# Projecting raw rows with centred weights, and applying 1/std afterwards, in a fused layer-norm, attention and expert kernel

## Chip, cores and metric

One core of a Trainium2 chip. The metric is the device time of one execution in microseconds (us). TensorE (PE) multiplies matrices and turns tiles, VectorE (DVE), ScalarE (ACT) and GpSimd (POOL) work on elements, SyncE (SP) issues most transfers.

## What is computed

The input is 8 sequences of 512 rows of 128. Each row is normalised; attention with 16 heads of 8 (causal, with a mask that depends on distance and head) and a mixture of 8 experts of which each row uses 2 are added to the row. Cut to what matters:

```python
def _layernorm(x, axis=-1, eps=1e-05):
    m = jnp.mean(x, axis=axis, keepdims=True)
    v = jnp.var(x, axis=axis, keepdims=True)
    return (x - m) / jnp.sqrt(v + eps)
...
qkv = x @ w_attn
...
logw = -jnp.log1p(decay[:, None, None] * log1p_dist)
attn_mask = causal[None, :, :] + logw
scores = jnp.einsum('bhqd,bhkd->bhqk', q, k) * (1.0 / jnp.sqrt(jnp.float32(D)))
att = jax.nn.softmax(scores + attn_mask[None], axis=-1)
...
logits = jnp.einsum('btd,ed->bte', x, Wr)
topk_vals, topk_idx = jax.lax.top_k(probs, TOPK)
h = jax.nn.silu(jnp.einsum('btd,efd->btef', x, W1))
...
xn = _layernorm(x, axis=-1)
x = x + attn(xn, ...) + ffn(xn, W1, W2, Wr)
```

## The kernel before

The rows lie in 32 tiles of 128, four to a batch. The attention works through 32 groups (8 batches of 4 groups of 4 heads) in a software pipeline of slots: `slot_steps(n)` lists the steps of slot n in one order, and each engine runs those that it has a function for, in that order. `PROLOGUE` is the list ahead of slot 0; `EARLY` and `EARLY_1` weave its remainder into slots 0 and 1, behind the score products of the group. Nothing else orders the engines but semaphores.

Steps by their two letters, with the lines that do them:

- BN, RS: mean and variance of tiles (VectorE, L942 and after), then 1/std as a power on GpSimd (L727), in three parts: batch 0, batches 1 to 3, batches 4 to 7.
- NX, NP: normalised rows `xn_all`, by VectorE for batches 0 and 4 to 7 (L959), by GpSimd for 1 to 3 (L734). The expert part sends these rows too.
- XB, VL: four normalised tiles of a batch are turned (L1210), copied by ScalarE (L815), and projected to values and expert logits (L1223), which ScalarE and VectorE copy (L820, L981). VS and XS store values and turned rows to DRAM; LC copies the logits (L741).
- KA, QA: keys and queries of a whole batch (L1250), split into three bf16 parts by ScalarE and VectorE (KR, KL, KM and the same with Q), written to DRAM (KW, QW) and loaded group by group (KD, QD), all of that on SP's queue.
- LN, CZ: the mask of a head, a logarithm on ScalarE (L809), and its causal edge for four heads on GpSimd (L748). The scores of group g wait for CZ g in the first four groups.
- P1: the score products of a group in ten units (L1266); VectorE takes the mask off and finds the row maximum (L1121); GpSimd subtracts for six units (L765) and ScalarE for the other four (SA, L846).
- TE: in slot n PE turns the ten units of group n - 1 (L1291) and ScalarE takes the exponentials (L884). `psT` has two buffers, so a turn waits for the exponential two before it. PV (L1309) multiplies with the values in slot n + 2 of group n, V brings the next batch's values (L870), OT, YT and PJ finish a batch.
- R1 to R17: choice of experts on VectorE in slots 2 to 12; SC sends rows to their expert's place on GpSimd (L776), the first choice in slots 8 to 18, the second in 20 to 30, three tiles a slot. MI, MU, MD run the 71 expert tiles behind the last slot.

## Time and profile before

| | |
|---|---|
| median of three runs | 531.16 us (529.22 to 532.96) |
| the profiled execution | 531.62 us, span 529.8 us, mean granted clock 0.974 |
| busy, share of the span | PE 91%, VectorE 68%, POOL 64%, ACT 63% |
| chain that ended last | PE 72%, VectorE 18%, POOL 3%, DMA 2%, ACT 2% |

Span is the stretch from the first to the last instruction on the profile; the 1.8 us beside it are the run's own. A group of instructions is given by source line, engine, operation, tile written and read, shape and count, with busy time and mean duration; a timeline row is start, duration, engine, line, operation and count, and in brackets the idle time before it with what released it. PEclk is the granted TensorE clock as a share of full speed.

### The profile page before, as it was taken

Reading aid. Unit: us, or ns where it says so; the run is one execution under the profiler, and the core shown is the slowest. Engines: PE = TensorE matmul, PEld = TensorE weight load, DVE = VectorE, ACT = ScalarE, POOL = GpSimd, SP = SyncE. Lnnn points to the kernel's source line nnn. Section 1 sums busy time; section 2 is a strip of 40 time slices with the busy share of each in tenths; the row PEclk is TensorE's granted clock in tenths of the full one; section 3 lists DMA queues with packets and bytes.
Section 4 is the critical chain, followed back from the end, with each engine's and each line's share of the span. In section 5 each row is a group of like instructions: output and inputs, shape, how many; then the busy total and the mean of one; then the engine's idle time right before and its main releaser. Section 6 shows DMA issues by size and latency. Waiting matters only on the chain.

```text
span 529.8 us, 13373 instructions
## 1 busy us (share of the span) xinstructions
PE 482.3 (91%) x4316; PEld 351.6 (66%) x4316; DVE 360.5 (68%) x1406; ACT 335.6 (63%) x600; POOL 338.4 (64%) x566
## 2 busy tenths in 40 slices
PE   7767999989999999999999999999999999999920
PEld 6545566555565665665565565666999999999910
DVE  7595997988988878888878878872433333333326
ACT  3578878878878878878878878776232333333300
POOL 2873555556888878876878888970454555555524
PEclk9988999999999999999999999999999999999975
DMA  6566591570460451450460451355466677666449
GB/s 179 168 232 207 156 219 47 157 214 8 136 185 23 135 173 36 137 164 23 136 181 27 137 165 50 107 171 141 121 201 190 209 215 207 207 183 207 131 166 319
DMA packets 71826, 80.38 MB, mean 152 GB/s; under 512 B 8638, under 2 KB 52672, under 8 KB 71760
## 3 DMA queue, kind: packets, MB, share of 16 engines
q1 hardware_dynamic: 67440, 71.06, 45.8%
q0 software_dynamic: 4320, 8.47, 4.5%
q8 instruction: 38, 0.62, 0.5%
q14 instruction: 28, 0.23, 0.1%
HBM read 48.11 MB, written 31.84 MB: 151 GB/s over the span
## 4 chain that ended last, share of the span: by engine, by line
PE 72%; DVE 18%; POOL 3%; DMA 2%; ACT 2%; issue 2%; SPq 0%; DVEq 0%; ACTq 0%; POOLq 0%
PE psT L1291 22%; PE psO L1309 13%; PE ps L1336 12%; DVE scores L1121 12%; PE psT L1363 12%; PE ps L1266 7%; PE psM L1250 2%; POOL xn_all L734 2%; DVE x_all L535 2%; PE ps L1327 1%; PE psM L1320 1%; DMA probs<-picked_dram 1%; POOL rstd L727 1%; ACT probs L884 1%; DMA decay_in<-decay_raw 1%
## 5 line engine op out<-in xcount | busy, mean ns | idle before, releaser
L1121 DVE CUSTOM_DVE_ANT_0 scores<-ps,wdist 128x256 f32<-128x256 f32 (+3 forms) x512 | 218.6, 486 | 28.1 <-PE ps L1266 25.4
L765 POOL TENSOR_SCALAR scores<-scores,row_max 128x256 f32<-128x256 f32 (+2 forms) x384 | 177.5, 477 | 62.9 <-DVE row_max L1121 61.6
L884 ACT ACTIVATE probs<-psT 128x512 f32<-128x512 f32 x320 | 173.7, 594 | 54.8 <-PE psT L1291 54.4
L1291 PE MATMUL psT<-ident,scores 128*128 128x128 f32 x1280 | 177.2, 281 | 3.4 <-ACT probs L884 2.8
L1291 PEld LDWEIGHTS psT<-ident,scores 128*128 128x128 f32 x1280 | 137.6, 141 | 63.7 <-issue 37.5
L783 POOL DMA_INDIRECT picked_dram<-scores,row_ring x71 | 69.7, 982 | 80.6 <-DVE scores L1173 79.1
L893 ACT ACTIVATE scores<-ps 128x512 f32<-128x512 f32 x71 | 42.4, 597 | 95.1 <-PE ps L1336 95.1
L846 ACT ACTIVATE scores<-scores,row_max 128x512 f32<-128x512 f32 x128 | 84.8, 714 | 0.0
L1309 PE MATMUL psO<-probs,values 128*32 128x512 f32 (+3 forms) x1024 | 82.0, 438 | 0.0
L1336 PE MATMUL ps<-scores,wdist 128*128 128x128 f32 x568 | 75.3, 276 | 0.8 <-DVE scores L1161 0.8
L1363 PE MATMUL psT<-wdist,scores 128*128 x568 | 75.3, 276 | 0.6 <-ACT scores L893 0.6
L776 POOL DMA_INDIRECT rows_dram<-xn_all x64 | 63.3, 989 | 16.2 <-issue 16.2
L1336 PEld LDWEIGHTS ps<-scores,wdist 128*128 128x128 f32 x568 | 69.1, 192 | 1.6 <-DVE scores L1161 1.2
L1363 PEld LDWEIGHTS psT<-wdist,scores 128*128 128x128 f32 x568 | 69.0, 192 | 1.1 <-issue 1.0
L1266 PE MATMUL ps<-k_rows,q_rows 48*128 48x256 bf16 (+3 forms) x512 | 57.8, 302 | 6.2 <-DVE row_max L1121 3.8
L1161 DVE COPY scores<-ps 128x128 f32<-128x128 f32 x71 | 20.6, 291 | 52.0 <-PE ps L1327 52.0
L1173 DVE TENSOR_SCALAR scores<-psT,row_ring 128x128 f32<-128x128 f32 x71 | 24.9, 351 | 43.8 <-PE psT L1363 43.8
L1309 PEld LDWEIGHTS psO<-probs,values 128*32 128x32 f32 x1024 | 25.5, 109 | 37.7 <-issue 28.5
L1121 DVE DVE_READ_ACCUMULATOR2_ANT row_max<- 128x1 f32 x512 | 42.1, 82 | 0.0
L1266 PEld LDWEIGHTS ps<-k_rows,q_rows 48*128 48x128 bf16 x512 | 17.1, 94 | 32.4 <-DVE row_max L1121 16.6
L1327 PE MATMUL ps<-ident,row_ring 128*128 128x128 f32 x71 | 19.2, 273 | 0.1
L535 DVE TENSOR_TENSOR x_all<-x_all,probs 128x512 f32<-128x512 f32 x12 | 11.1, 927 | 8.5 <-DMA probs<-picked_dram 8.1
(140 smaller groups left out, 277.4 us busy)
## 6 DMA issues: line engine op xcount, KB each, us to landing
wdist<-w1t SPq DMA_DIRECT2D x71, 256.0 KB, 3.2
k_rows<-k_dram SPq DMA_DIRECT2D x64, 96.0 KB, 2.8
q_rows<-q_dram SPq DMA_DIRECT2D x64, 96.0 KB, 2.6
row_ring<-rows_dram SPq DMA_DIRECT2D x71, 65.0 KB, 3.0
probs<-picked_dram SPq DMA_DIRECT2D x8, 512.0 KB, 6.8
rows_dram<-row_ring SPq DMA_DIRECT2D x7, 585.0 KB, 5.8
k_dram<-k_parts SPq DMA_DIRECT2D x7, 384.0 KB, 2.3
q_dram<-q_parts SPq DMA_DIRECT2D x7, 384.0 KB, 2.6
```

Source lines behind the costliest of these rows:

```text
L765: last = nc.gpsimd.tensor_scalar(part, part, -1.0, row_max[:, r, tile, quad:quad + 1], ALU.mult, ALU.add)
L776: nc.gpsimd.indirect_dma_start(out=rows_dram, out_offset=bass.IndirectOffsetOnAxis(ap=xn_all[:, t, 0:1].bitcast(U32), axis=0), in_=xn_all[ ...
L783: nc.gpsimd.indirect_dma_start(out=picked_dram, out_offset=bass.IndirectOffsetOnAxis(ap=slot_rows[s % RING][:, 0:1].bitcast(U32), axis=0), ...
L846: nc.scalar.activation(part, part, ACT.Identity, scale=-1.0, bias=row_max[:, r, TILES - 1, quad:quad + 1]).then_inc(less_act, 1)
L884: nc.scalar.activation(probs[:, at.ring(2), w, :], psT[:, w % 2], ACT.Exp, scale=-1.0).then_inc(exp_ready, 1)
L893: nc.scalar.activation(hidden_t[:, s % 2], ps1[:, s % 2], ACT.Silu).then_inc(hidden_ready, 1)
L1121: last = nc.vector.tensor_tensor_reduce(out=scores[:, r, u, col:col + n], in0=bank[:, col:col + n], in1=wdist[:, at.g * QUADS + quad, SEQ ...
L1266: last = mm(ps1[:, 2 * (step % 2) + strip, col:col + n], q_rows[a:a + HEAD_ROWS, at.ring(4), pair, tile * P:n], k_rows[a:a + HEAD_ROWS, at ...
L1291: last = nc.tensor.transpose(psT[:, w % 2, place * P:(place + 1) * P], scores[:, at.ring(2), u, col + key * P:col + (key + 1) * P], ident[:])
L1309: last = mm(psO[quad * QROWS:(quad + 1) * QROWS, tile * P:], values[:, at.parity, tile, first:first + QROWS], probs[:, at.ring(2), unit, a ...
L1336: last = mm(ps1[:, s % 2, f * P:(f + 1) * P], slot_w1[s % RING][:, f * P:(f + 1) * P], slot_xt[:, s % 2], start=True, stop=True)
L1363: last = mm(psT[:, s % 2, 0:C], hidden_t[:, s % 2, f * P:(f + 1) * P], w2[:, bass.ds(start + f * C, C)], start=(f == 0), stop=(f == FT - 1))
```

## The change

The rows of batches 1 to 7 are no longer normalised before they are turned and projected. The weights (now one array with the expert router's) are centred once: PE multiplies them by identity minus 1/128 (WC), which takes the mean off every row that is projected. 1/std comes in as a factor later: turned rows are multiplied by a broadcast row of it on VectorE (XN) before keys and queries; values when ScalarE brings them in (four instructions, one a tile); logits on GpSimd in LC. For that, 1/std is turned on PE (RT), copied, stored to DRAM (RO) and loaded back for all partitions into `yt` (RB). The rows for the experts are normalised on GpSimd in slots 3 to 8, five tiles a slot (NR), and the sends begin in slot 9.

With it: projections get banks of their own (`vl_banks`), six of eight projections stand in the prologue, the second query write moves to GpSimd's queue (QP), GpSimd subtracts all ten units in slots 0 to 2, and logarithms 8 to 15 move behind the third score product of slots 1 and 2. The table of `log_dist` moves to the last part of `probs`, which is why the last exponential of slot 2 waits for all masks. Core of the diff:

```diff
...
-FIRST_SEND_SLOT = 8
...
-EARLY = {0: (("VL", 12), ("LN", 4), ("LN", 5)),
-         1: (("NX", 16), ("VS", 12), ("LC", 4), ("LN", 6), ("LN", 7), ("CZ", 1)),
-         2: (("XB", 16), ("XS", 16), ("NX", 20), ("LC", 8), ("LN", 8), ("LN", 9)),
-         3: (("VL", 16), ("XB", 20), ("XS", 20), ("VS", 16), ("NX", 24), ("LC", 12), ("LN", 10), ("LN", 11), ("CZ", 2)),
-         4: (("VL", 20), ("XB", 24), ("XS", 24), ("VS", 20), ("NX", 28), ("LC", 16), ("LN", 12), ("LN", 13))}
-EARLY_1 = (("VL", 24), ("XB", 28), ("XS", 28), ("VS", 24), ("LC", 20), ("LN", 14), ("LN", 15), ("CZ", 3), ("VL", 28),
-           ("VS", 28), ("LC", 24), ("LC", 28))
+EARLY = {0: {1: (("VL", 24), ("LN", 4), ("LN", 5)),
+             2: (("VL", 28), ("LN", 6), ("LN", 7)) + tuple(("LC", b * GROUPS) for b in range(6)),
+             3: (("RT", 1), ("V0", 0), ("XN", 4), ("LC", 24), ("LC", 28), ("CZ", 1)),
+             4: tuple((kind, b * GROUPS) for kind, b in (("VS", 4), ("VS", 5), ("XS", 3), ("VS", 6), ("VS", 7), ("XS", 4))
+                      ) + (("RO", 1), ("XS", 20), ("XS", 24), ("XS", 28))},
+         1: {2: (("LN", 8), ("LN", 9)), 3: (("LN", 10), ("LN", 11), ("CZ", 2))},
+         2: {2: (("LN", 12), ("LN", 13)), 3: (("LN", 14), ("LN", 15), ("CZ", 3))}}
+FIRST_ROWS_SLOT, ROW_TILES = 3, 5
...
+GROUPS_BY_POOL = 3
...
+def act_units(c):
+
+    return ACT_UNITS if c >= GROUPS_BY_POOL else ()
...
+    per_batch("XT", -4)
+    per_batch("RB", -4)
...
-    step("SA", n, NGROUP, (0, 1))
+    if n >= GROUPS_BY_POOL:
+        step("SA", n, NGROUP, (0, 1))
...
-    per_batch("XT", -4)
     p1(4)
+    per_batch("XN", -4)
     step("TE", n - 1, NGROUP, 8, 10)
-    step("SA", n, NGROUP, (6, 7))
+    if n >= GROUPS_BY_POOL:
+        step("SA", n, NGROUP, (6, 7))
+    first = TILES + ROW_TILES * (n - FIRST_ROWS_SLOT)
+    if TILES <= first < NTILE:
+        steps.append(("NR", 0, first, min(NTILE, first + ROW_TILES)))
...
 PROLOGUE = [
-    ("BN", 0, 0, 0, 4), ("RS", 0, 0), ("NX", 0), ("WU", 18), ("XB", 0), ("KA", 0), ("QA", 0), ("WU", 16),
-    ("BN", 0, 1, 4, 16), ("RS", 0, 1), ("NP", 4), ("NP", 8), ("NP", 12),
-    ("KR", 0), ("QR", 0), ("KM", 0), ("QM", 0), ("LN", 0), ("LN", 1),
-    ("KL", 0), ("QL", 0), ("KW", 0, 0), ("QW", 0, 0), ("KD", 0), ("QD", 0), ("KW", 0, 1), ("QW", 0, 1),
-    ("VL", 0), ("XB", 4), ("LN", 2), ("LN", 3), ("CZ", 0),
-    ("BN", 0, 2, 16, 20), ("BN", 0, 2, 20, 24), ("VL", 4), ("XB", 8), ("XS", 8),
-    ("BN", 0, 2, 24, 28), ("VL", 8), ("XB", 12), ("XS", 12), ("BN", 0, 2, 28, 32), ("RS", 0, 2),
-    ("V0", 0), ("VS", 4), ("VS", 8), ("LC", 0)]
-MISC_KINDS = ("KA", "QA", "VL", "PJ", "CT")
+    ("BN", 0, 0, 0, 4), ("RS", 0, 0), ("WU", 10), ("WC", 0), ("WU", 6), ("NX", 0), ("XB", 0), ("XB", 4), ("KA", 0), ("QA", 0),
+    ("BN", 0, 1, 4, 16), ("RS", 0, 1),
+    ("KR", 0), ("QR", 0), ("KM", 0), ("QM", 0), ("KL", 0), ("QL", 0), ("XB", 8), ("VL", 0),
+    ("KW", 0, 0), ("QW", 0, 0), ("KD", 0), ("QD", 0), ("QP", 0),
+    ("XB", 12), ("VL", 4), ("RT", 0), ("LN", 0), ("LN", 1), ("BN", 0, 2, 16, 20),
+    ("XB", 16), ("VL", 8), ("LN", 2), ("LN", 3), ("CZ", 0), ("BN", 0, 2, 20, 24),
+    ("XB", 20), ("VL", 12), ("BN", 0, 2, 24, 28),
+    ("XB", 24), ("VL", 16), ("BN", 0, 2, 28, 32), ("RS", 0, 2),
+    ("XB", 28), ("VL", 20),
+    ("RO", 0), ("KW", 0, 1), ("RB", 4), ("VS", 4), ("VS", 8), ("XS", 8), ("VS", 12)]
+MISC_KINDS = ("KA", "QA", "PJ", "CT")
...
+        def vl_banks(b):
+
+            if b > 5:
+                return psO, psM
+            return (ps1[:, 0], ps1[:, 1]) if b % 2 == 0 else (psO, ps1[:, 3])
...
-                sp.dma_start(w_qkv[:, 0:3 * C], w_attn).then_inc(w_loaded, 16)
+                sp.dma_start(w_qkv[:], w_attn).then_inc(w_loaded, 16)
...
-                    if n == 0:
-                        sp.dma_start(w_qkv[:, 3 * C:], wrt).then_inc(consts_dma, 16)
...
+                def rstd_store(at):
+                    n = at.c
+                    sp.wait_ge(rstd_copied, n + 1)
+                    sp.dma_start(rstd_dram[n * NTILE // 2:(n + 1) * NTILE // 2], rstd_stage(n)).then_inc(rstd_stored, 16)
+
+                def scales_load(at):
+                    b = at.c // GROUPS
+                    sp.wait_ge(rstd_stored, 16 if b < 4 else 32)
+                    if b == 2:
+                        sp.wait_ge(xt_scaled, 1)
+                    if b >= 3:
+                        sp.wait_ge(misc_full, at.misc_before("PJ", 3 * GROUPS, 1))
+                    sp.dma_start(yt[:], rstd_dram[b * TILES:(b + 1) * TILES].rearrange("(a t) p -> a (t p)", a=1
+                                                                                     ).broadcast_to([P, SEQ])
+                                 ).then_inc(scales_loaded, 16)
...
-                    elif at.g == 0 or at.c == 1:
-                        sp.wait_ge(q_written, at.batches(48, 48))
+                    elif at.c == 1:
+                        sp.wait_ge(q_by_pool, 48)
+                    elif at.g == 0:
+                        sp.wait_ge(q_written, at.batches(48))
...
+                pool.wait_ge(ident_ready, 1)
+                nc.gpsimd.tensor_scalar(centre, ident[:], 1.0, -1.0 / C, ALU.mult, ALU.add).then_inc(centre_ready, 1)
...
-                def normalise_step(at):
...
+                def rows_step(at, first, end):
+
+                    for t in range(first, end):
+                        nc.gpsimd.tensor_scalar(xn_all[:, t, 3:], x_all[:, t, :], mean[:, t:t + 1], rstd[:, t:t + 1],
+                                                ALU.subtract, ALU.mult).then_inc(rows_normal, 1)
...
+                    pool.wait_ge(rstd_ready, 3)
+                    scale = rstd[:, b * TILES:(b + 1) * TILES].rearrange("p (t a) -> p t a", a=1)
+                    nc.gpsimd.tensor_tensor(dst, v_stage(b)[:, :, C:], scale.broadcast_to([P, TILES, EXPERTS]), ALU.mult
+                                            ).then_inc(logits_ready, 1)
...
+                def queries_write(at):
+                    write_queries(nc.gpsimd, pool, at, 1, q_by_pool)
...
+                run_prologue({"RS": rstd_step, "QP": queries_write, "CZ": causal_step})
...
+                        pool.wait_ge(rows_normal, NTILE - TILES)
...
+                def centred_copy(at):
+                    act.wait_ge(centred_full, 1)
+                    nc.scalar.activation(w_qkv[:], ps1[:, 0, 0:3 * C + EXPERTS], ACT.Copy).then_inc(centred_copied, 1)
...
+                    act.wait_ge(rstd_ready, 3)
...
-                    nc.scalar.activation(value_cols[:, at.parity, :, :, 0:HD],
-                                         v_back[:, :, 0:C].rearrange("p t (h d) -> p t h d", d=HD),
-                                         ACT.Copy).then_inc(values_ready, 1)
+                    for t in range(TILES):
+                        tile = at.batches(TILES, t)
+                        last = nc.scalar.activation(value_cols[:, at.parity, t, :, 0:HD],
+                                                    v_back[:, t, 0:C].rearrange("p (h d) -> p h d", d=HD),
+                                                    ACT.Copy, scale=rstd[:, tile:tile + 1])
...
+                        if at.c == 1 and w == UNITS - 1:
+                            act.wait_ge(wdist_ready, HEADS)
...
+                def scaled_weights(at):
+                    dve.wait_ge(centred_copied, 1)
+                    v.tensor_scalar(w_q[:], w_qkv[:, 0:C], SCALE, None, ALU.mult).then_inc(w_q_ready, 1)
...
+                def scale_tokens(at):
+
+                    b = at.c // GROUPS
+                    dve.wait_ge(scales_loaded, 16 * b)
+                    if b == 1:
+                        dve.wait_ge(xt_copied, 2)
+                        dve.wait_ge(vl_full, 2)
+                    else:
+                        dve.wait_ge(xt_loaded, 16 * (b - 1))
+                    v.tensor_tensor(xt[:, at.parity, :], xt[:, at.parity, :], yt[:], ALU.mult).then_inc(xt_scaled, 1)
...
+                    dve.wait_ge(rows_normal, at.batches(TILES))
...
-                    if b in POOL_NORMS:
...
+                    if b == 0:
+                        pe.wait_ge(xn_ready, 1)
...
-                        pe.wait_ge(xn_ready, 1 if b == 0 else b - 2)
+                        pe.wait_ge(x_loaded[b // TILES], 16)
...
-                        last = nc.tensor.transpose(xt_bank(b)[:, t * P:(t + 1) * P], xn_all[:, b * TILES + t, 3:], ident[:])
+                        tile = xn_all[:, t, 3:] if b == 0 else x_all[:, b * TILES + t, :]
+                        last = nc.tensor.transpose(xt_bank(b)[:, t * P:(t + 1) * P], tile, ident[:])
...
+                def centre_weights(at):
+
+                    pe.wait_ge(centre_ready, 1)
+                    pe.wait_ge(w_loaded, 16)
+                    mm(ps1[:, 0, 0:3 * C + EXPERTS], centre, w_qkv[:], start=True, stop=True).then_inc(centred_full, 1)
...
+                def rstd_turn(at):
+
+                    n = at.c
+                    pe.wait_ge(rstd_ready, n + 2)
+                    pe.wait_ge(vo_free, BATCH if n else 2)
+                    nc.tensor.transpose(psO[0:NTILE // 2, SEQ - P:], rstd[:, n * NTILE // 2:(n + 1) * NTILE // 2], ident[:]
+                                        ).then_inc(rstd_turned, 1)
...
+                    if b >= 2:
+                        pe.wait_ge(vo_free, b if b > 5 else b - 1)
+                        pe.wait_ge(vm_free, b - 1 if b < 7 else b)
...
+                        pe.wait_ge(centred_copied, 1)
+                    if b == 3:
+                        pe.wait_ge(rstd_copied, 1)
+                    if b == 6:
+                        pe.wait_ge(misc_free, 1)
...
-                        if kind == "KA" and (at.c >= 2 * GROUPS):
-                            pe.wait_ge(xt_loaded, at.batches(16, -16))
+                        if kind == "KA" and at.c > 0:
+                            pe.wait_ge(xt_scaled, at.batches(1))
...
+                    if step == 0:
+                        pe.wait_ge(vo_free, 5)
+                        pe.wait_ge(vm_free, 5)
+                    if step == 1:
+                        pe.wait_ge(vm_free, 6)
+                        pe.wait_ge(misc_free, MISC["QA", 0] + 1)
...
```

## Rows read from the trace of the kernel before

**Rows 1.** Windows: stretch, length, busy us PE PEld DVE ACT POOL, PEclk, DMA, GB/s

```profile
200.00:300.00 100.00, 98.82 (x910) 59.49 (x909) 84.80 (x354) 83.97 (x154) 81.00 (x148) 1.00 0.32 101
```

**Rows 2.** Chain of waits, opening: start us, us, what

```profile
26.36 2.93 POOL rstd L727
```

**Rows 3.** Timeline of PE, opening and slots 0 to 3

```profile
11.81 1.02 PE L1250 MATMUL ps<-xt,w_q 128*128 128x512 f32 x2
...
22.84 0.73 PE L1223 MATMUL psO<-w_qkv,probs 128*128 128x136 f32 x4 [0.69 <-ACT probs L815]
...
24.59 0.66 PE L1210 MATMUL psT<-ident,xn_all 128*128 128x128 f32 x4 [0.56 <-POOL xn_all L734]
25.18 0.39 PE L1266 MATMUL ps<-k_rows,q_rows 48*128 48x512 bf16 x2
...
43.06 1.09 PE L1291 MATMUL psT<-ident,scores 128*128 128x128 f32 x8
...
48.54 3.69 PE L1291 MATMUL psT<-ident,scores 128*128 128x128 f32 x16 [1.02 <-ACT probs L884]
...
65.37 1.09 PE L1291 MATMUL psT<-ident,scores 128*128 128x128 f32 x8
66.39 1.71 PE L1309 MATMUL psO<-probs,values 128*32 128x512 f32 x16
```

**Rows 4.** Timelines of GpSimd, SP's queue and PE, last slots

```profile
356.37 1.85 POOL L765 TENSOR_SCALAR scores<-scores,row_max 128x384 f32<-128x384 f32 x4 [1.25 <-DVE row_max L1121]
...
357.80 5.58 SPq L652 DMA_DIRECT2D row_ring<-rows_dram  x8
...
365.23 0.38 PE L1327 MATMUL ps<-ident,row_ring 128*128 128x128 f32 x2
```

**Rows 5.** Timeline of ScalarE, opening and first exponentials

```profile
19.09 0.60 ACT L815 ACTIVATE xt<-psT 128x512 f32<-128x512 f32 x1 [1.32 <-PE psT L1210]
19.58 1.32 ACT L809 ACTIVATE wdist<-probs,decay 128x512 f32<-128x512 f32 x2
20.97 0.40 ACT L820 ACTIVATE probs<-psO 128x272 f32<-128x272 f32 x1
...
43.82 1.28 ACT L884 ACT_TABLE_LOAD   x1 [0.58 <-PE psT L1291]
45.12 1.08 ACT L884 ACTIVATE probs<-psT 128x512 f32<-128x512 f32 x2
```

**Rows 6.** Timeline of SP's queue, second key write

```profile
19.63 2.56 SPq L601 DMA_DIRECT2D k_dram<-k_parts  x3
```

**Rows 7.** Page, groups of instructions and one DMA issue

```profile
L1121 DVE CUSTOM_DVE_ANT_0 scores<-ps,wdist 128x256 f32<-128x256 f32 (+3 forms) x512 | 218.6, 486 | 28.1 <-PE ps L1266 25.4
...
L884 ACT ACTIVATE probs<-psT 128x512 f32<-128x512 f32 x320 | 173.7, 594 | 54.8 <-PE psT L1291 54.4
...
L776 POOL DMA_INDIRECT rows_dram<-xn_all x64 | 63.3, 989 | 16.2 <-issue 16.2
...
row_ring<-rows_dram SPq DMA_DIRECT2D x71, 65.0 KB, 3.0
```

**Rows 8.** Timeline of GpSimd, opening

```profile
24.50 0.63 POOL L748 TENSOR_SCALAR_AFFINE_SELECT wdist<-wdist 128x512 f32<-128x512 f32 x1
...
29.24 0.21 POOL L741 COPY logits<-probs 128x32 f32<-128x32 f32 x1
29.45 1.94 POOL L765 TENSOR_SCALAR scores<-scores,row_max 128x384 f32<-128x384 f32 x4
```

**Rows 9.** Groups by shape, first 60 us, GpSimd

```profile
L734 POOL TENSOR_SCALAR xn_all<-x_all,mean,rstd 128x128 f32<-128x128 f32 x12 | 9.3, 784 | 0.1
...
L765 POOL TENSOR_SCALAR scores<-scores,row_max 128x384 f32<-128x384 f32 x10 | 5.9, 593 | 5.4 <-DVE row_max L1121 5.4
```

**Rows 10.** Windows view, two stretches around an idle PE, columns as in rows 1

```profile
28.00:30.00 2.00, 0.00 (x0) 0.00 (x0) 1.95 (x10) 2.00 (x5) 2.00 (x3) 1.00 0.94 294
...
32.00:34.00 2.00, 1.85 (x8) 1.38 (x7) 2.00 (x9) 1.79 (x3) 2.00 (x6) 0.50 0.91 276
```

More of the change, by code:

```diff
@@ L110 @@
 ACT_UNITS = (0, 1, 6, 7)
-POOL_UNITS = tuple(u for u in range(UNITS) if u not in ACT_UNITS)
+GROUPS_BY_POOL = 3
 FILLS = 8
@@ L124, in score_place, with pool_units, units_done @@
     return 2 * i + strip, {3: 0, 2: 0, 0: 384, 1: pair * 256}[tile]
+def act_units(c):
+    return ACT_UNITS if c >= GROUPS_BY_POOL else ()
+def pool_units(c):
+    return tuple(u for u in range(UNITS) if u not in act_units(c))
+def units_done(units, c, ready):
+    return sum(len(units(k)) for k in range(c)) + sum(u < ready for u in units(c))
 def probs_place(tile, quad):
@@ L157, in p1 @@
         route(i)
-        if n == 0:
-            steps.extend(EARLY.get(i, ()))
-        if n == 1 and i == 0:
-            steps.extend((kind, c - n) for kind, c in EARLY_1)
+        steps.extend((kind, c - n) for kind, c in EARLY.get(n, {}).get(i, ()))
     if n == NGROUP + 1:
@@ L541, in part_rows, with write_queries @@
             return dst[at.parity].rearrange("(r k) s -> r k s", k=KINDS)[some]
+        def write_queries(engine, eng, at, part, written):
+            eng.wait_ge(misc_free, at.misc("QA", 1))
+            some = head_rows(at, part)
+            rows = part_rows(q_dram, at, some)
+            for part_no, (first, n) in enumerate(((0, 3), (3, 2), (5, 1))):
+                engine.dma_start(rows[:, first:first + n],
+                                 q_parts[some, part_no:part_no + 1].broadcast_to([some.stop - some.start, n, SEQ])
+                                 ).then_inc(written, 16)
         def head_rows(at, first):
@@ L604, in queries_write @@
                 def queries_write(at, part=1):
[L605 to L611 removed]
+                    write_queries(sp, sp, at, part, q_written if part else q_first)
                 def rows_load(dst, src, at, loaded):
@@ L1276, in turn_step @@
                         ready = (6, UNITS)[pair]
[L1277 to L1278 removed]
+                        pe.wait_ge(less_max, units_done(pool_units, at.c, ready))
+                        if at.c >= GROUPS_BY_POOL:
+                            pe.wait_ge(less_act, units_done(act_units, at.c, ready))
                         if at.c == 0 and w == 0:
```

125 lines of the change are left out of this document (67 added, 58 removed).

## Prediction

> **What bounds the kernel now.** I read the windows view first, for the middle of the run. TensorE (PE) is busy 98.82 of 100 us there, VectorE, ScalarE and GpSimd 81 to 85 [rows 1], so in a normal slot only PE counts. Nothing of the change lies on PE in such a slot; what it can win or lose lies where PE waits, that is at the opening, and I read the rest for that.
>
> The chain of waits shows what the opening hangs on: GpSimd takes 2.93 us for the last 1/std, from 26.36 us [rows 2]. Normalisation by VectorE, turning, copying and projecting the last four batches follow it, in between the scores of group 0. PE's timeline gives the length: the scores of group 0 begin at 25.18 us and the first turn of slot 1 (L1291, the step that ends a slot's waits) comes at 43.06 [rows 3]. So slot 0 is 18 us long. From the first turn of slot 3, at 65.37, to the tokens of the expert part, at 365.23, lie 30 slots [rows 3, 4]: 299.9 / 30 = 10.0 us each. Some 8 us of slot 0 are thus there to be won, and this is what the change goes for. I follow both milestones, first turn of slot 1 and first turn of slot 3; what comes behind the second is the same work.
>
> **Up to slot 0.** The waits for normalised rows go. PE has its last query projection done at 11.81 + 1.02 = 12.8 [rows 3]. Then come six batches of four transposes (0.66) and eight projections (0.73 for four, so about 1.3) [rows 3]: 6 x 1.96 = 11.8, so the first score product stands at about 24.8 against 25.18. ScalarE's copies of a batch (0.60 and 0.40) and four logarithms (1.32 for two) [rows 5] are 8.6 us in those 11.8, hidden; without that cover they would add what exceeds it. The centring product and its copy lie before the first row is normalised; the added store and broadcast of 1/std sit in SP's queue ahead of the second key write, which took 2.56 us from 19.63 [rows 6]. With them that write is issued by 22.6, lands by 25.6 (3.0 us for a load, row_ring [rows 7]) and lets the loads of group 1 go, there by about 30.5; group 1 wants them at 31.5 or later. I cost both at nothing. The second query write goes to GpSimd's queue. No row shows a plain transfer issued there; the nearest is an indirect send at 0.99 us [rows 7]. Three of these are 3 us, between 15.5, when the lowest part of the queries is there, and the first mask at about 20.8, after ScalarE's four logarithms (both worked out as above); if each of its 576 lines cost what a send's 128 do (4.5 us) it would just fit.
>
> **Slot 0.** VectorE now has one group's scores (218.6 / 32 = 6.8 us [rows 7]), two copies of 0.4 and the product with 1/std (a unit's 0.68): 8.3 us, from 25.3 to 33.6. GpSimd is later. The statistics of the last sixteen tiles end when the fourth last projection is copied, at about 25.0 rather than 26.3, and the 1/std takes 2.93 [rows 2], so it is free at 27.9. It now turns all ten units, not six. A pair of units of 384 + 128 costs 1.94 [rows 8]; one of 512 I put at 0.70, between 0.593 for 384 and 0.79 in proportion [rows 9]. Units 0 to 5: 1.4 + 1.9 + 1.9 = 5.3, at 33.2. The first turn of slot 1 needs these six and the score products ahead of it on PE: **33.8 instead of 43.06, 9.3 us won.**
>
> **Slots 1 and 2.** Here the gain meets a cost. GpSimd goes on: six logits at 0.2, units 6 and 7, two logits, mask 0.63 [rows 8], done at 36.8, and VectorE waits for that mask before slot 1's scores. Four units (2.7) and the rest of the keys (0.7) bring it to 40.2; ScalarE's middle part of the keys (0.60) ends at 40.8. The new order then puts four logarithms (LN 8 to 11) between exponentials 3 and 4. In the trace the first exponential after the logarithms starts only behind a table load, 43.82 to 45.12 with 1.28 us in it [rows 5]. The same must happen twice in slot 1 and twice in slot 2, four loads that were not there before, 5.1 us. A hole in the exponentials is 1.28 + 2.64 + 1.28 = 5.2 us, and PE's turns 6 to 9 and its last score product wait for exponential 4. In slot 1 this ends at 40.8 + 5.2 + 0.5 = 46.5, PE having finished turn 5 at about 40.5: 6 us idle. Four turns (1.09 for two [rows 3]) and three score products follow: first turn of slot 2 at 49.7.
>
> In slot 2 PE has two turns, the query projection (1.02), half the values product (1.71) and two turns [rows 3], 4.9 us, at 54.6. Exponential 3 and the middle part end at 55.8, the hole at 61.0, exponential 4 at 61.5, PE's rest 3.2 us later: first turn of slot 3 at 64.7. Before it was 65.37. So 9.3 us won at the first milestone shrink to **0.7 at the second**: the two slots take 30.9 us, not 22.3. That ScalarE is spared four units a slot in slots 0 to 2 does not help, since the hole, not its sum, is what PE waits for.
>
> **TensorE's clock.** In the trace PE was idle from 28 to 30 us, and at 32 to 34 the granted clock was 0.50, the lower of its two levels (1.2 GHz, not 2.4) [rows 10]. It came again at 48.54, where 16 transposes took 3.69 us; at 1.09 for eight they would be 2.1 [rows 3]: 1.6 us. The new order has two holes of 4 to 6 us, so two such stretches, between 0 (the low clock falls into the hole) and 1.7 each. I take half: +1.6.
>
> **Later slots.** The product with 1/std is 0.68 us of VectorE in six later slots, 0 to 4.1; it sits behind the last scores of a slot in which VectorE has no outputs to turn, and VectorE is 15% idle [rows 1]: +0.2. The values copy becomes four of at most 0.40 [rows 5], up to 1.0 more on ScalarE, seven times; before exponentials ScalarE was idle 54.8 us in all [rows 7], 1.7 a slot: +0.3, at most 7. GpSimd's rows: 28 x 0.784 [rows 9], five a slot are 3.9 beside six units at 5.7, 9.6 of 10.0: nothing, while the next slot's turns come after its units; if that slack is gone it is the second rival. Sends move a slot later. The second list of places is written in the middle of slot 20, and VectorE waits there for sends issued at the end of slot 19; before, a projection wait covered that: +0.3, up to 1. The last two sends now follow the last units of slot 31, 356.37 + 1.85 + 2 x 0.99 = 360.2 [rows 4, 7], where before the loads of rows could go at 357.80 and the first rows were used at 365.23 [rows 4]. With about 2.5 us for the sends to land and 3.0 for a load [rows 7] that is 365.7: +0.7, from 0 to 3.
>
> **Sum.** 531.62 (span 529.8 and 1.8 around it) - 0.7 + 1.6 + 0.2 + 0.3 + 0.3 + 0.7 = 534.0. The median of the runs shown, 531.16, lies 0.5 below that profiled execution, so I say **533.5**. About 1% (5.3 us) is what a measurement of this kernel can tell from no change.
>
> **Rivals.** First, faster: the added loads do not appear, because one table serves both functions. For it speaks nothing in the trace; against it the load at 43.82, after a stretch of logarithms [rows 5]. The holes would be 2.6 us, the end 5.1 earlier, with less idling and its clock loss gone too: 526 to 528, and 523 if GpSimd also takes fewer than 5.3 us for its first six units. With what other errors of the opening would do the same, 0.18. The Trainium skill, ScalarE: Activation LUTs, section Table sets: the hidden batching unit, says that a set exists which holds both exp and ln, so that ln and then exp need one load; by that rule the time would be this rival's, and the trace, loading again, does not agree.
>
> Second, slower: GpSimd becomes the bound in slots 3 to 8. It decides when five rows and six units, with the waits between, exceed a slot: 9.6 us of work against 10.0, and before, it waited for VectorE's scores three times a slot. If its rows do not fit into those waits, each of the six slots grows by about 0.8: 534 + 5 = 539. For it: the small margin; against it: units 0 to 5 are wanted only in the next slot. 0.13.
>
> Third, slower: dearer holes. At the low clock for their full 1.7 us each, and last sends that land 3 us late, 531.6 - 0.7 + 3.4 + 0.8 + 3 = 538. 0.12. The Trainium skill, ScalarE: Activation LUTs, section What ACT_TABLE_LOAD costs, puts a switch at about 2.66 us, a drain included; four would then cost 10.6 and not 5.1, and the time would be 539. The trace does not agree: from load to exponential it shows 1.30 us [rows 5].
>
> **Chances.** No change within 1%: 0.57, its own range 529 to 537. Faster 0.18, slower 0.25 (0.13 + 0.12). The range is 525 to 540: below lies the first rival at its best, above both slower ones together.
>
> **What would show it.** Table loads on ScalarE, two each in slots 1 and 2, four more than before. First turn of slot 1 near 34, and two holes in the turns there of 4 to 6 us. First turn of slot 3 near 65. GpSimd's last mask-gated unit, not VectorE, releasing slot 1. Wrong would be: no added loads; a first turn after 36; PE waiting for GpSimd's units in slots 3 to 8; first expert tokens more than 2 us after the last turn.

## The result: 539.34 us against 530.84, slower by 1.7%

The changed kernel took 539.34 us (median of 4 runs, 537.01 to 541.10), the kernel before, beside it, 530.84 (529.22 to 532.96). The ratio is 1.0169, 95% interval 1.0137 to 1.0201. Measured again later beside the last experiment it was 1.0154 (1.0116 to 1.0193). The profiled executions: 538.57 us with a span of 536.8 after, 531.62 with 529.8 before, so 7.0 us of span to explain. The forecast of 533.5 us, no change within 1%, did not come true; the time lies at the upper end of its range, where the third rival stood.

What the change set out to win, it won. GpSimd's timeline of the changed kernel (start us, us, engine, line, operation, tiles) at the opening:

```profile
23.53 2.93 POOL L800 TENSOR_TENSOR rstd<-var_eps,minus_half 128x16 f32<-128x16 f32 x1 [2.18 <-DVE var_eps L1035]
26.48 5.45 POOL L846 TENSOR_SCALAR scores<-scores,row_max 128x512 f32<-128x512 f32 x10
...
34.80 0.62 POOL L829 TENSOR_SCALAR_AFFINE_SELECT wdist<-wdist 128x512 f32<-128x512 f32 x1
```

The last 1/std still takes 2.93 us, as in [rows 2], but turning and projecting the rows no longer wait for it; six units (5.45 us for their ten instructions) follow and end at 31.93, and the second mask ends at 35.42. TensorE's timeline, the lines that answer to [rows 3]:

```profile
32.84 0.61 PE L1408 MATMUL ps<-k_rows,q_rows 48*128 48x512 bf16 x6 [2.39 <-DMA q_rows<-q_dram]
33.38 1.60 PE L1434 MATMUL psT<-ident,scores 128*128 128x128 f32 x8
...
38.59 1.09 PE L1434 MATMUL psT<-ident,scores 128*128 128x128 f32 x8
...
45.30 1.94 PE L1434 MATMUL psT<-ident,scores 128*128 128x128 f32 x8 [5.62 <-ACT probs L985]
...
47.72 1.97 PE L1434 MATMUL psT<-ident,scores 128*128 128x128 f32 x8
...
50.59 1.22 PE L1434 MATMUL psT<-ident,scores 128*128 128x128 f32 x8
...
62.43 1.94 PE L1434 MATMUL psT<-ident,scores 128*128 128x128 f32 x8 [4.75 <-ACT probs L985]
...
67.70 1.19 PE L1434 MATMUL psT<-ident,scores 128*128 128x128 f32 x8
```

The first turn of slot 1 comes at 33.38 instead of 43.06: 9.7 us won. GpSimd's six units were done by then; the last wait before it is that of the score products ahead of it, 2.39 us for the queries of group 1. Then two holes, 5.62 and 4.75 us, and the first turn of slot 3 comes at 67.70 instead of 65.37. Slots 1 and 2 took 34.3 us, before 22.3. ScalarE's timeline shows what is in a hole, here the first:

```profile
38.79 0.60 ACT L958 ACTIVATE k_parts<-psM 128x512 bf16<-128x512 f32 x1
39.40 1.28 ACT L892 ACT_TABLE_LOAD   x1
40.70 2.56 ACT L892 ACTIVATE wdist<-probs,decay 128x512 f32<-128x512 f32 x4
43.27 1.28 ACT L985 ACT_TABLE_LOAD   x1
44.56 1.08 ACT L985 ACTIVATE probs<-psT 128x512 f32<-128x512 f32 x2
```

Load, four logarithms, load: 5.1 us between two exponentials, with TensorE waiting for the second. And the windows view (columns as in [rows 1]) shows the granted clock behind each hole:

```profile
40.00:42.00 2.00, 0.00 (x0) 0.00 (x0) 1.94 (x7) 1.99 (x4) 2.00 (x6) 1.00 0.97 277
...
46.00:48.00 2.00, 2.00 (x12) 1.26 (x11) 0.18 (x1) 1.19 (x2) 0.00 (x0) 0.50 0.92 175
...
64.00:66.00 2.00, 2.00 (x12) 1.30 (x11) 1.06 (x5) 0.75 (x3) 0.18 (x1) 0.50 0.46 115
```

TensorE is idle at full granted clock from 40 to 42, and works without a pause at 0.50 (1.2 of 2.4 GHz) from 46 to 48: eight turns take 1.94 or 1.97 us there and 1.09 at 38.59. At the end of the run, in the timelines of GpSimd, SP's queue and TensorE, the lines that answer to [rows 4]:

```profile
362.63 1.01 POOL L858 DMA_INDIRECT rows_dram<-xn_all  x1 [0.15 <-issue]
363.95 0.96 POOL L858 DMA_INDIRECT rows_dram<-xn_all  x1 [0.30 <-issue]
...
369.32 3.66 SPq L723 DMA_DIRECT2D row_ring<-rows_dram  x8
...
371.33 0.72 PE L1473 MATMUL ps<-ident,row_ring 128*128 128x128 f32 x2 [1.69 <-DMA row_ring<-rows_dram]
372.02 2.08 PE L1482 MATMUL ps<-scores,wdist 128*128 128x128 f32 x8
```

The last two sends stand behind the last units of slot 31; SP starts the row loads 4.4 us after the second was issued (363.95 + 0.96), and TensorE waits 1.69 us for rows.

**Where the 7 us came from.** The table was worked out from TensorE's timelines: for each slot the start of its first product with the values (L1309 before, L1453 after), in us for the kernel before and as a difference to it for the others. A step from one row to the next is what those slots lost. The columns e1 to e6 and e10 are experiments below.

| slot | before | changed | e1 | e2 | e3 | e4 | e5 | e6 | e10 |
|---|---|---|---|---|---|---|---|---|---|
| 2 | 56.31 | -3.72 | -7.41 | -5.33 | +0.15 | -6.93 | -8.56 | -9.54 | -0.67 |
| 3 | 66.39 | +2.43 | -7.04 | -4.09 | +5.97 | -6.56 | -6.96 | -8.55 | +5.48 |
| 5 | 88.30 | +2.92 | -6.55 | -3.60 | +6.46 | -6.07 | -5.32 | -8.06 | +5.97 |
| 9 | 130.24 | +3.91 | -5.58 | -2.17 | +9.46 | -4.37 | -4.34 | -8.05 | +8.87 |
| 11 | 149.78 | +3.91 | -5.58 | -2.17 | +11.62 | -1.06 | -4.34 | -7.84 | +8.87 |
| 20 | 240.19 | +3.91 | -5.58 | -2.17 | +11.61 | -1.05 | -4.35 | -7.85 | +8.86 |
| 21 | 250.40 | +4.22 | -5.26 | -1.86 | +11.60 | -1.06 | -4.05 | -7.86 | +9.17 |
| 32 | 357.94 | +4.25 | -5.24 | -1.83 | +11.62 | -1.06 | -4.04 | -7.86 | +9.19 |
| 33 | 366.98 | +7.04 | -3.23 | -0.36 | +11.62 | -1.06 | -4.04 | -7.86 | +9.19 |

For the changed kernel that reads: +2.4 up to slot 3, +0.5 in slot 3 (row 3 to row 5), +1.0 in slots 5 to 8, +0.3 in slot 20, +2.8 at the end.

### The profile page after: what moved, and what is told of

The parts are those of the page before. It is cut to its first block, busy times and chain, and to the rows that moved or that the text cites. A ratio compares the mean times of both kernels' runs of the same rounds, so it can differ in the third digit from the quotient of the medians.

```text
span 536.8 us, 13385 instructions
## 1 busy us (share of the span) xinstructions
PE 482.5 (90%) x4284; PEld 350.9 (65%) x4284; DVE 360.4 (67%) x1397; ACT 338.2 (63%) x616; POOL 366.2 (68%) x598
## 4 chain that ended last, share of the span: by engine, by line
PE 70%; DVE 16%; DMA 4%; ACT 4%; issue 2%; POOL 2%; SPq 1%; DVEq 0%; POOLq 0%
PE psT L1434 20%; PE psO L1453 12%; PE ps L1482 12%; PE psT L1509 12%; DVE scores L1235 11%; PE ps L1408 7%; PE psM L1386 2%; DVE x_all L584 2%; PE ps L1473 2%; DMA rows_dram<-xn_all 1%; PE psM L1466 1%; DMA probs<-picked_dram 1%; POOL scores L846 1%; DMA v_dram<-probs 1%; ACT wdist L892 1%
## 5 line engine op out<-in xcount | busy, mean ns | idle before, releaser
L846 POOL TENSOR_SCALAR scores<-scores,row_max 128x384 f32<-128x384 f32 (+3 forms) x396 | 189.4, 492 | 43.4 <-DVE row_max L1235 42.1
L1434 PE MATMUL psT<-ident,scores 128*128 128x128 f32 x1280 | 179.9, 284 | 12.6 <-ACT probs L985 11.6
L1434 PEld LDWEIGHTS psT<-ident,scores 128*128 128x128 f32 x1280 | 140.0, 143 | 73.9 <-issue 52.3
L1453 PE MATMUL psO<-probs,values 128*32 128x512 f32 (+3 forms) x1024 | 82.5, 441 | 0.0
L938 ACT ACTIVATE scores<-scores,row_max 128x512 f32<-128x512 f32 x116 | 77.0, 714 | 0.0
L1453 PEld LDWEIGHTS psO<-probs,values 128*32 128x32 f32 x1024 | 25.6, 110 | 38.2 <-issue 30.1
L806 POOL TENSOR_SCALAR xn_all<-x_all,mean,rstd 128x128 f32<-128x128 f32 x28 | 22.6, 815 | 0.0
```

The source lines that it names most:

```text
L846: last = nc.gpsimd.tensor_scalar(part, part, -1.0, row_max[:, r, tile, quad:quad + 1], ALU.mult, ALU.add)
L938: nc.scalar.activation(part, part, ACT.Identity, scale=-1.0, bias=row_max[:, r, TILES - 1, quad:quad + 1]).then_inc(less_act, 1)
L1434: last = nc.tensor.transpose(psT[:, w % 2, place * P:(place + 1) * P], scores[:, at.ring(2), u, col + key * P:col + (key + 1) * P], ident[:])
L1453: last = mm(psO[quad * QROWS:(quad + 1) * QROWS, tile * P:], values[:, at.parity, tile, first:first + QROWS], probs[:, at.ring(2), unit, a ...
```

## Experiments

Theory 1: the holes, that is table loads and logarithms between exponentials, and the low clock behind them ate the gain of the opening. Theory 2: the end is late because the last sends are. Rivals: something else bounds slots 1 and 2; the loss of slots 5 to 8 lies with ScalarE's four value copies or VectorE's added product, or with GpSimd's rows. Every kernel below is the changed one with the edit that is shown.

### e1: logarithms 8 to 15 in slot 0

```diff
-EARLY = {0: {1: (("VL", 24), ("LN", 4), ("LN", 5)),
-             2: (("VL", 28), ("LN", 6), ("LN", 7)) + ...
+EARLY = {0: {1: (("LN", 4), ("LN", 5), ("LN", 6), ("VL", 24), ("LN", 7), ("LN", 8), ("LN", 9)),
+             2: (("VL", 28), ("LN", 10), ("LN", 11)) + ...
-             3: (... ("LC", 28), ("CZ", 1)),
+             3: (... ("LC", 28), ("CZ", 1), ("LN", 12), ("LN", 13), ("LN", 14), ("LN", 15)),
-         1: {2: (("LN", 8), ("LN", 9)), 3: (("LN", 10), ("LN", 11), ("CZ", 2))},
-         2: {2: (("LN", 12), ("LN", 13)), 3: (("LN", 14), ("LN", 15), ("CZ", 3))}}
+         1: {3: (("CZ", 2),)},
+         2: {3: (("CZ", 3),)}}
```

> The changed kernel with the eight logarithms of masks 2 and 3 (LN 8 to 15) moved from slots 1 and 2 into slot 0, where ScalarE was idle 2.28, 1.93 and 2.92 us before copies and the first exponential; nothing else moves. Theory 1 (the two holes in the exponentials and the low clock that follows them ate the gain of the opening): four table loads of 1.28 us and both holes of PE (5.62 and 4.75 us) are gone, the first turn of slot 3 comes at 56 to 59 us instead of 67.70, and the kernel takes 527 to 531 us against 539.3 of the changed one. Rival (something else, VectorE's scores or GpSimd's ten units, holds slots 1 and 2 at over 13 us each): the first turn of slot 3 stays above 63 and the time above 535.

Measured: 527.99 us, ratio to before 0.9961 (0.9944 to 0.9978), 11 us below the changed kernel. ScalarE's and TensorE's timelines:

```profile
34.15 2.54 ACT L892 ACTIVATE wdist<-probs,decay 128x512 f32<-128x512 f32 x4
37.94 1.28 ACT L985 ACT_TABLE_LOAD   x1 [1.25 <-PE psT L1434]
...
43.52 1.11 PE L1434 MATMUL psT<-ident,scores 128*128 128x128 f32 x8 [0.34 <-ACT probs L985]
...
44.92 1.11 PE L1434 MATMUL psT<-ident,scores 128*128 128x128 f32 x8
...
58.33 1.09 PE L1434 MATMUL psT<-ident,scores 128*128 128x128 f32 x8
```

The last four logarithms now end before the one table load at which the exponentials begin. The turns that stood behind the first hole wait 0.34 us and run at full clock, and slot 3 begins at 58.33. From the first turn of slot 1 (36.72 in this execution) that is 21.6 us for two slots, against 34.3. Theory 1 holds; nothing else bounds these slots at 13 us.

### e2: an exponential in place of each of these logarithms

```diff
-nc.scalar.activation(wdist[:, h, :], log_dist, ACT.Ln, bias=1.0, ...
+nc.scalar.activation(wdist[:, h, :], log_dist, ACT.Ln if h < 8 else ACT.Exp, bias=1.0, ...
```

> The changed kernel with the function of the eight logarithms in slots 1 and 2 replaced by an exponential at the same place (so masks 2 and 3, heads 8 to 15, hold other numbers; count, shapes and order of the instructions stay). Only the table loads go. Theory 1 in parts: if the loads are what counts, the holes shrink by 2 x 1.28 us each, 5.1 us in all, and about 1 to 2 us of low clock with them: 532 to 534.5 us, first turn of slot 3 at 61 to 63. If the place of the logarithms alone makes the hole (turns held for other reasons), the time stays at 538 to 539.

Measured: 531.53 us (529.31 to 536.32 in ten runs), ratio 1.0041 (1.0007 to 1.0076). ScalarE's and TensorE's timelines:

```profile
41.39 2.57 ACT L892 ACTIVATE wdist<-probs,decay 128x512 f32<-128x512 f32 x4
43.84 1.09 ACT L985 ACTIVATE probs<-psT 128x512 f32<-128x512 f32 x2
...
44.59 1.11 PE L1434 MATMUL psT<-ident,scores 128*128 128x128 f32 x8 [2.73 <-ACT probs L985]
```

No load, a hole of 2.73 instead of 5.62 us, and the first eight turns behind it at full clock; a shorter stretch at the low clock follows (granted clock 0.52 from 46 to 48, 0.62 from 48 to 50). The first turns of slots 1 and 3 come at 35.78 and 61.28: 25.5 us. So of the 12.7 us between the changed kernel's 34.3 and e1's 21.6, 8.8 belong to four loads (5.1 by their durations) with the low clock that went with them, and 3.9 to the place of the logarithms themselves, with that stretch.

### e3 and e4: sends from slot 8, without and with the logarithms of e1

```diff
-FIRST_SEND_SLOT = 9
+FIRST_SEND_SLOT = 8
```

> The changed kernel with the sends of rows begun one slot earlier, in slot 8 as before the change (they still wait for 28 normalised rows). Theory 2 (the tail of 2.8 us is the last sends landing after the last turns): row loads go at about 358 us of the unchanged clock of slots, first tokens follow the turns, low clock in the tokens is gone, and the slot 20 wait of 0.3 us too: 535.5 to 537 us. Rival (the tail comes from elsewhere, or slot 8 with its normalised rows, units and sends overruns and gives it back): 538.5 or more.

> Both moves together: logarithms in slot 0, sends from slot 8. If the two losses are independent, as theories 1 and 2 have it, the gains add: 524 to 528 us, below both kernels. What is left over the opening's gain would then be the 1 to 1.5 us lost in slots 3 to 8. If one covers the other (GpSimd late everywhere), it is not better than the first of these runs.

Measured: 540.80 us (ratio 1.0187, 1.0155 to 1.0220) and 530.78 (1.0004, 0.9980 to 1.0028). Both miss: no gain from e3, and e4 is 2.8 us slower than e1. The table tells why. The end lost nothing in either (rows 32 and 33 are equal) and slot 20 neither, as theory 2 has it. But between slots 9 and 11 e4 lost 3.3 us and e3 2.2. VectorE's, GpSimd's and TensorE's timelines of e4 there:

```profile
132.36 5.66 POOL L846 TENSOR_SCALAR scores<-scores,row_max 128x384 f32<-128x384 f32 x12
...
134.85 2.93 DVE L1257 TENSOR_TENSOR y_q<-o_q,rden 128x256 f32<-128x256 f32 x1
...
136.08 1.97 PE L1434 MATMUL psT<-ident,scores 128*128 128x128 f32 x8 [1.83 <-POOL scores L846]
```

In slot 8 GpSimd normalises three rows and sends three on top of its six units, falls behind, and then does twelve instructions without a pause, from 132.36 to 138.02. TensorE waits 1.83 us for its units, and turns at the low clock afterwards (eight turns in 1.97 us, not 1.09; granted clock 0.50 from 136 to 138). So GpSimd is the bound at this place, and the wait and the low clock behind it are e4's 3.3 us. In the same stretch VectorE's product y_q, 0.48 us elsewhere, takes 2.93 and ends at 137.78, just before the stretch does; TensorE has no wait behind it. That gave theory 4: while GpSimd works without a pause, it holds certain VectorE instructions up; its rows in slots 3 to 8 do the same on a smaller scale.

### e6: rows filled, not normalised

The edit to e4:

```diff
-nc.gpsimd.tensor_scalar(xn_all[:, t, 3:], x_all[:, t, :], mean[:, t:t + 1], rstd[:, t:t + 1],
-                        ALU.subtract, ALU.mult).then_inc(rows_normal, 1)
+nc.gpsimd.memset(xn_all[:, t, 3:], 0.0).then_inc(rows_normal, 1)
```

> e4_logs_and_sends with the normalisation of rows in slots 3 to 8 replaced by a fill with zeros of the same tiles (the expert rows of batches 1 to 7 are zero; number, order and signals of the instructions stay). Theory 4 (GpSimd without a pause holds VectorE's instructions up: y_q took 2.93 instead of 0.48 us at 134.85): the 3.3 us that e4 lost between the second products of slots 9 and 10 are gone, y_q there is back at 0.5, the small instructions of slots 4 to 8 (ends, places, pick) are as short as before the change, and most of the 1.7 us lost between slots 4 and 9 goes too: 525 to 527 us, 4 to 5 below e4. Rival (the sends in slot 8, or the moved instructions on ScalarE and VectorE, make the loss): slots 9 to 10 stay 13 us apart.

Measured: 525.02 us in one execution, span 523.3 against e4's 530.1. The edit changes two things at once: a fill takes GpSimd 0.20 us, a row took 0.79 (medians of 28), so GpSimd also has less to do. The small instructions on VectorE that add up the experts' ends in slot 5, first in the changed kernel, behind them GpSimd's line of that moment, then the same two instructions in e6:

```profile
97.19 0.41 DVE L1164 COPY ends_b<-ends_a 128x2 f32<-128x2 f32 x1
97.52 0.54 DVE L1165 TENSOR_TENSOR ends_b<-ends_a 128x6 f32<-128x6 f32 x1
...
94.63 3.71 POOL L846 TENSOR_SCALAR scores<-scores,row_max 128x384 f32<-128x384 f32 x8
```

```profile
86.20 0.17 DVE L1163 COPY ends_b<-ends_a 128x2 f32<-128x2 f32 x1
86.27 0.16 DVE L1164 TENSOR_TENSOR ends_b<-ends_a 128x6 f32<-128x6 f32 x1
```

0.41 and 0.54 us go back to 0.17 and 0.16. At the end of that slot TensorE waits for VectorE's row maxima, in the changed kernel, in e6 and in the kernel before:

```profile
100.57 0.39 PE L1408 MATMUL ps<-k_rows,q_rows 48*128 48x384 bf16 x4 [1.45 <-DVE row_max L1235]
```

```profile
88.86 0.39 PE L1407 MATMUL ps<-k_rows,q_rows 48*128 48x384 bf16 x4 [0.72 <-DVE row_max L1234]
```

```profile
96.91 0.39 PE L1266 MATMUL ps<-k_rows,q_rows 48*128 48x384 bf16 x4 [0.72 <-DVE row_max L1121]
```

In slots 6 and 7 the same wait is 0.80 and 0.86 us in the changed kernel, 0.68 and 0.73 in the other two. In the table e6 loses nothing from slot 5 to slot 9, where the other columns lost about 1.0 or more, and 0.2 instead of 3.3 between slots 9 and 11. (y_q is not quite back: 0.98 us once in that stretch, behind three sends.) For the 1.0 us of slots 5 to 8 theory 4 holds: the rows push GpSimd's units (94.63 to 98.34) onto VectorE's small instructions, and TensorE waits for VectorE. For the 3.3 us of slots 9 to 11 it is not shown: there TensorE waited for GpSimd itself, and e6 shortens GpSimd's work too. The Trainium skill, SBUF — State Buffer, section SBUF: two separate sides, says that VectorE, in an instruction with two SBUF inputs, and GpSimd, in one that reads SBUF, share a pair of ports that one of them holds for a whole instruction while the other blocks. The traces agree, and show more: y_q waited through several GpSimd instructions of about 0.5 us, almost to the end of their unbroken stretch.

### e7 and e8: the two other suspects for slots 3 to 8

The edits to e1, values in one copy without the factor, and one column of tokens scaled:

```diff
-for t in range(TILES):
-    last = nc.scalar.activation(value_cols[:, at.parity, t, :, 0:HD], ..., ACT.Copy, scale=rstd[:, tile:tile + 1])
+last = nc.scalar.activation(value_cols[:, at.parity, :, :, 0:HD], ..., ACT.Copy)
```

```diff
-v.tensor_tensor(xt[:, at.parity, :], xt[:, at.parity, :], yt[:], ALU.mult)
+v.tensor_tensor(xt[:, at.parity, 0:1], xt[:, at.parity, 0:1], yt[:, 0:1], ALU.mult)
```

> e1_logs_in_slot0 with the four scaled copies of the values of a batch made one unscaled copy again (the values of batches 1 to 7 miss the factor 1/std). If the three extra instructions cost 0.6 us of ScalarE where PE waits for it, the shift of 0.49 us between slots 3 and 4 against before goes and about 0.5 us of span with it, perhaps 0.1 more at slots 7 to 8; else the shifts stay as in e1_logs_in_slot0.

> e1_logs_in_slot0 with the product of the turned tokens with 1/std cut to one column of 512 (queries and keys of batches 2 to 7 miss the factor), so its place and its waits stay and 0.6 us of VectorE go in slots 4, 8, 12 and so on. If VectorE's 0.69 us is behind part of the loss in slots 4 to 9 (0.73 between slots 5 and 6), that part goes: 0.3 to 0.7 us of span. If GpSimd's rows alone make that loss, the shifts stay as in e1_logs_in_slot0 within 0.2.

Measured, one execution each: 529.92 and 529.23 us. By the table's measure e7 stays at -8.85 from slot 3 to slot 5, where e1 went from -7.04 to -6.55: the four copies cost the 0.5 us, once, in slot 3. e8 loses 1.63 from slot 3 to slot 9, e1 1.46: the added product of VectorE has no part in it. But e7 as a whole did not gain; from slot 5 to slot 6 it lost 2.3 us where e1 lost 0.7. TensorE's timelines of e7, then e1, at that place:

```profile
88.80 0.39 PE L1405 MATMUL ps<-k_rows,q_rows 48*128 48x384 bf16 x4 [1.46 <-DVE row_max L1232]
89.12 1.84 PE L1431 MATMUL psT<-ident,scores 128*128 128x128 f32 x8
```

```profile
91.10 0.39 PE L1408 MATMUL ps<-k_rows,q_rows 48*128 48x384 bf16 x4 [1.46 <-DVE row_max L1235]
91.42 1.09 PE L1434 MATMUL psT<-ident,scores 128*128 128x128 f32 x8
```

The same wait of 1.46 us; behind it eight turns take 1.84 us in e7 and 1.09 in e1. The granted clock fell in one (0.58 and 0.57 in the two windows from 89 to 93 us) and not in the other (1.00 in both from 91 to 95), which is the rest of the 2.3.

### e5: the second list's sends from slot 20, with the logarithms of e1

```diff
-pick = int(n > SECOND_PICK_SLOT)
-first = SENDS * (n - (SECOND_PICK_SLOT + 1 if pick else FIRST_SEND_SLOT))
+pick = int(n >= SECOND_PICK_SLOT)
+first = SENDS * (n - (SECOND_PICK_SLOT if pick else FIRST_SEND_SLOT))
```

> Logarithms in slot 0 as in e1_logs_in_slot0, sends from slot 9 as in the change, but the sends of the second list begin at the end of slot 20, the slot in whose middle that list is written, instead of slot 21; so the last two sends lie in slot 30, as before the change, and slot 8, where rows are normalised, has no sends. Theory 2 in its new form (the tail is the last sends, and the earlier repair failed only because slot 8 was overfull): row loads go at about 348 to 350 us, not 359.01, the first tokens follow the turns, 2.0 us of tail are gone and no slot grows: 525 to 526.5 us against 527.99. Rival (slot 20, with list and sends, overruns as slots 8 and 9 did): 528 or more, the loss visible between slots 20 and 22.

Measured: 525.65 us, ratio 0.9894 (0.9850 to 0.9938), as theory 2 expected and clear of e1's interval. The timelines of SP's queue and TensorE:

```profile
353.78 5.60 SPq L723 DMA_DIRECT2D row_ring<-rows_dram  x8
...
361.20 0.38 PE L1473 MATMUL ps<-ident,row_ring 128*128 128x128 f32 x2
```

Rows are there when the turns end, and the tokens run at full clock (0.38 us, as in [rows 4], not 0.72). The end loses nothing; slot 20 keeps its 0.3. This version beats both kernels.

### e9: rows between the units

The edit to e5, where `rows(a, b)` puts the rows a to b - 1 of a slot's five:

```diff
     p1(2)
+    rows(0, 2)
     p1(3)
+    rows(2, 4)
...
-    steps.append(("NR", 0, first, min(NTILE, first + ROW_TILES)))
+    rows(4, ROW_TILES)
```

> e5_second_list_slot20 with the five rows that GpSimd normalises per slot split up: two after the third pair of units, two after the fourth, one at the end of the slot, so that GpSimd has no stretch of 4 us behind its last units. Theory 4 (the loss of 0.7 to 1.7 us in slots 4 to 9 comes from VectorE's instructions held up while GpSimd works without a pause): less of it, 0.5 to 1 us gained, 524.5 to 525.5 us against 525.65. Rival: rows between the units delay the units themselves, which the next products and turns wait for; 526 or more, PE waiting for GpSimd's units in slots 4 to 9.

Measured: 525.44 us, ratio 0.9891 (0.9840 to 0.9942), which can't be told from e5. From slot 5 to slot 9 it lost 0.88 us, e5 0.98. Splitting the rows gives no relief that can be seen; the expectation of 0.5 to 1 us was wrong. The two small instructions of slot 5 are shorter in its profile (0.31 and 0.15 us), but y_q there takes 0.91 instead of 0.48.

### e10, e11 and e12: the end alone, on the changed kernel

e10 and e12 are the changed kernel with the edit of e5 alone; e11 is the changed kernel unedited.

> The changed kernel with nothing but the second list's sends begun in slot 20. Theory 2: the tail of 2.8 us goes and slot 8 is not touched: 536 to 537.5 us against 539.3, the table loads and holes of slots 1 and 2 unchanged. Rival (what e5_second_list_slot20 gained over e1_logs_in_slot0 was the scatter of the opening): 538.5 or more.

> The changed kernel as it is, beside the next one, to see how far its opening scatters: the profiles so far show the first turn of slot 1 at 33.38 us in one execution of it and at 36.76 us in e10_only_second_list, whose opening is the same. Theory: the opening of the changed kernel scatters by some 3 us from one execution to the next, with the arrival of the first queries; the median of many runs is 538.5 to 541 us and a second profile may show the first turn of slot 3 at 67 to 71 us.

> e10_only_second_list once more, against the changed kernel on the same chip. Theory 2 (tail): over many runs it lies 2 to 3 us below the changed kernel, since only the end of slot 31 is different. Rival (the first four runs, which lay 1 us above it, tell the truth: the tail's gain is given back in the expert part): equal within 1 us, with the expert part, from first tokens to the end, longer than the 165.5 us of the changed kernel by what the tail lost less.

Measured: e10 540.40 us (ratio 1.0177, 1.0124 to 1.0230); side by side, e11 537.46 (1.0154, 1.0116 to 1.0193) and e12 538.25 (1.0141, 1.0113 to 1.0169). No gain in time can be seen, against theory 2's 2 to 3 us. In the profiles the end does what it should. TensorE's timelines of e11, then e12:

```profile
370.71 0.60 PE L1473 MATMUL ps<-ident,row_ring 128*128 128x128 f32 x2 [0.91 <-DMA row_ring<-rows_dram]
```

```profile
372.96 0.38 PE L1473 MATMUL ps<-ident,row_ring 128*128 128x128 f32 x2
```

e11 loses 1.1 us at the end (by the table's measure +4.40 in slot 32, +5.50 in slot 33), less than the 2.8 of the first profile, in which the granted clock was 0.50 from 372 to 374 (e11: 1.00); e10 and e12 lose none. In the profiles the opening hides it, which none of these edits touches. The windows view of the changed kernel, then of e10:

```profile
32.00:34.00 2.00, 1.16 (x11) 0.88 (x12) 0.96 (x8) 0.00 (x0) 2.00 (x8) 0.95 1.11 342
```

```profile
32.00:34.00 2.00, 1.33 (x7) 0.24 (x6) 2.00 (x5) 1.60 (x4) 2.00 (x7) 0.50 1.14 329
```

In the profiles of the changed kernel and e11 the clock was near full at 32 to 34 and the first turn of slot 1 came at 33.38 and 33.49; in e10 and e12 it was at 36.76 and 36.64 (the clock stood at 0.50 through that stretch, and in e10 and e12 from 28 to 40), and 3 us of that are left at slot 3. The first queries arrive at different times, too: the first score product stands at 23.15, 24.46, 25.35 and 25.21 in these four. e2, with the sends of the changed kernel, also opens late (35.78), and so does e3 (37.71). Whether it is chance that all three profiles with earlier sends on this opening show the later one stays open, and with it what the end is worth on the changed kernel: 1.1 to 2.8 us by its profiles, nothing by its times. The rival, a longer expert part that gives the gain back, is not seen: from the first tokens to the end 166.0 us in e10 and 163.8 in e12, 165.5 in the changed kernel and 164.5 in e11.

## Why the prediction was right and wrong

- **The opening** came out as said, in part by luck. First turn of slot 1: 33.8 said, 33.38 measured, with the second mask of GpSimd at 35.42 (36.8 said) behind it. But the sum ends with GpSimd's six units, at 33.2, and they were done at 31.93. What came last was a load costed at nothing, the queries of group 1, "there by about 30.5", which TensorE waited for until 32.84 (2.39 us; 2.42 in e11). Two errors cancelled. (A slip beside it: 12.8 + 11.8 is 24.6, not 24.8, for the first score product; 23.15 measured.) In the profiles of the experiments the first turn came between 33.49 and 37.71, in six of the twelve after the 36 that the prediction named as a sign of being wrong, a scatter that the prediction, made from one execution, did not see.
- **The holes** were right: two table loads each in slots 1 and 2, 1.28 us each, two holes of 4 to 6 us said, 5.62 and 4.75 measured. e1 removes them and brings the two slots to 21.6 us, 22.3 in the kernel before. The first rival, no added loads, is thereby refuted in the changed kernel; e2 shows what it would have been worth, 531.5 us and not 526 to 528. Its hole of 2.73 us is as said (2.6); but in its profile the first turn of slot 1 came at 35.78, and slots 3 to 9, slot 20 and the end lost 3.7 us (-4.09 to -0.36 in the table), where the sum had 1.5.
- **The clock behind the holes is the first step that failed**, in size. "I take half: +1.6" should have been the upper bound or a little over it. From the end of the first hole to the first turn of slot 2 the changed kernel needs 50.59 - 45.30 = 5.3 us, e1 for the same work 3.5 (43.52 to 47.02); behind the second hole it needs 5.3, e2 3.3 (57.96 to 61.28). That is 3.7 us, not 1.6. The low clock did not fall into the hole: the granted clock is 1.00 from 42 to 44, 0.51 from 44 to 46, where the hole ends, and 0.50 from 46 to 50, under the work behind it.
- **Slots 3 to 9 are the second term that was mis-sized**: 0.2 + 0.3 said, 1.5 measured. The value copies cost 0.5 (e7) and VectorE's product nothing (e8); the missing 1.0 is from the rows on GpSimd. The prediction costed those at nothing because GpSimd's work fits its slot, and up to slot 7 it does: GpSimd still waits for VectorE once in each of slots 5 to 7 (1.58, 1.16 and 1.24 us). The second rival (GpSimd the bound, each slot longer by 0.8) did not happen in the changed kernel either: TensorE's one wait there that is put down to GpSimd, 0.54 us in slot 3, is put down to ScalarE in e1 and is gone in e7. The rival's mechanism shows in e3 and e4, where sends come on top of rows. What neither counted is that work on one engine lengthens instructions on another.
- **The second list**: 0.3 said, 0.31 measured in slot 20.
- **The end is the third term that was mis-sized**: +0.7 said with 0 to 3 as bounds (365.7 against 365.23 is 0.5 by its own terms); 2.8 and 1.1 in two profiles of the changed kernel, 1.5 to 2.4 in e1, e2, e7 and e8, and nothing in the seven profiles whose sends end a slot earlier. The sends took 4.4 us from issue to the row loads, where 2.5 was assumed, and TensorE, once it waits 1.7 us, also does the first tokens at the low clock, which the sum did not carry.
- **The choice among the cases.** The sum added 2.4 us to the span; the parts measured are 2.4 (up to slot 3) + 1.5 + 0.3 + 2.8 = 7.0. The third rival, holes at the full price of the low clock and sends that land late, was put at 538 with a chance of 0.12, and it is what happened, with the rows' loss on top. The forecast had taken each of its two parts at half or less: 1.6 of 3.4 for the clock, 0.7 of 3 for the sends.
